# A macaron transformer block: the row maxima of two heads in one reduction, one of four transposed copies on VectorE, and the query/key rounding issued between two heads' exponentials

## The reference, cut to what matters

```python
# x: (32, 256, 128); ffn: H=16 heads, DH=64, E=8 experts, top-2
def ffn(x):                        # x already layer-normed
    q = einsum('btc,hdc->bhtd', x, Wq);  k = einsum('btc,hdc->bhtd', x, Wk)
    mix_v = top2_sigmoid_weights(einsum('btc,hec->bthe', x, Ws))
    v = einsum('bthe,bted->bhtd', mix_v, einsum('btc,edc->bted', x, Wv))
    probs = softmax(einsum('bhid,bhjd->bhij', q * DH**-0.5, k))
    attn = einsum('bhij,bhjd->bihd', probs, v)
    mask_o = top2_mask(einsum('btc,hec->bthe', x, Wd))
    return einsum('bthe,bthd,efd->bthf', mask_o, attn, Wo).sum(axis=2)
x = x + 0.5 * ffn(layernorm(x))
x = x + linear_attention(layernorm(x))      # states from k and v, out, layer norm, Wo
x = x + 0.5 * ffn(layernorm(x))
```

## Time and profile before

| | us |
|---|---|
| median of 3 runs | 2554.22 |
| the runs | 2555.17, 2553.99, 2554.22 |
| profiled execution, its own time | 2555.17 |
| its span | 2553.4 |
| granted TensorE clock, mean | 0.993 |

### The profile page before, as it was taken

One profiled execution on the slowest core, in us unless ns is written; L12 is line 12 of the kernel. 1 busy time (PEld: TensorE's weight loads), 2 busy tenths in 40 slices (PEclk: granted clock), 3 DMA queues, 4 the chain that ended last, 5 costly groups with the idle time before them and its releaser, 6 DMA issues.

```text
span 2553.4 us, 111659 instructions
## 1 busy us (share of the span) xinstructions
PE 2469.9 (97%) x45824; PEld 2321.9 (91%) x45824; DVE 1983.8 (78%) x3498; ACT 2073.2 (81%) x6373; POOL 1138.9 (45%) x1126
## 2 busy tenths in 40 slices
PE   4999999999999999999999999999999999999997
PEld 3899999999999999999999999999999999999997
DVE  4787777778877778888788787788787788887874
ACT  3888888888888888888888888888888888888885
POOL 2354545445445345344445354454453453444431
PEclk8999999999999999999999999999999999999998
DMA  4555555655656656555555556556556556556553
GB/s 130 149 154 147 144 146 140 163 151 153 162 147 158 158 152 157 146 164 148 157 159 155 155 150 166 149 154 164 146 155 158 153 157 157 152 145 156 162 155 99
DMA packets 519351, 387.58 MB, mean 152 GB/s; under 512 B 214080, under 2 KB 436160, under 8 KB 510656
## 3 DMA queue, kind: packets, MB, share of 16 engines
q1 hardware_dynamic: 518416, 379.60, 55.5%
q10 hardware_dynamic: 432, 0.85, 0.1%
HBM read 191.64 MB, written 188.74 MB: 149 GB/s over the span
## 4 chain that ended last, share of the span: by engine, by line
PE 80%; ACT 10%; issue 5%; DVE 3%; POOL 1%; DMA 1%; SPq 0%; ACTq 0%; DVEq 0%; POOLq 0%
PE psT L451 16%; PE psS L408 15%; PE psS L490 7%; PE psT L490 7%; ACT PB L758 7%; PE psT L468 6%; PE psT L470 5%; PE psT L469 5%; PE psT L463 5%; PE psT L421 5%; PE psT L435 4%; DVE NMAX L639 2%; ACT PT L846 1%; ACT QK L767 1%; DVE QK L698 1%
## 5 line engine op out<-in xcount | busy, mean ns | idle before, releaser
L758 ACT ACTIVATE PB<-psS,NMAX 128x256 f32<-128x256 f32 x2048 | 943.5, 488 | 246.5 <-DVE NMAX L639 246.5
L451 PE MATMUL psT<-V,PT 128*64 128x64 f32 x16384 | 540.4, 224 | 7.3 <-issue 7.1
L451 PEld LDWEIGHTS psT<-V,PT 128*64 128x64 f32 x16384 | 502.4, 138 | 35.1 <-issue 10.0
L698 DVE TENSOR_TENSOR QK<-psT,QK 128x512 fp32r<-128x512 f32 x512 | 341.1, 688 | 211.4 <-ACT QK L767 209.3
L639 DVE TENSOR_REDUCE NMAX<-psS 128x2 f32<-128x512 f32 x512 | 329.6, 685 | 202.9 <-PE psS L408 202.4
L758 ACT ACTIVATION_READ_ACCUMULATOR PB<-psS,NMAX 128x1 f32 x2048 | 452.6, 221 | 0.0
L408 PE MATMUL psS<-QK 64*128 64x256 f32 x6144 | 434.7, 286 | 14.8 <-ACT PT L846 13.1
L408 PEld LDWEIGHTS psS<-QK 64*128 64x128 f32 x6144 | 389.6, 186 | 63.5 <-issue 63.3
L767 ACT ACTIVATE QK<-psT 128x512 fp32r<-128x512 f32 x512 | 298.7, 622 | 84.1 <-PE psT L470 69.4
L864 POOL TENSOR_TENSOR BT<-MT,diagv 128x1024 f32<-128x1024 f32 x128 | 308.4, 2410 | 118.0 <-DMA MT<-MIXd 118.0
L641 DVE TENSOR_REDUCE NMAX<-psS 128x4 f32<-128x1024 f32 x256 | 310.9, 1214 | 0.0
(11 more groups left out here) (119 smaller groups left out, 4582.2 us busy)
## 6 DMA issues: line engine op xcount, KB each, us to landing
Vd<-VM SPq DMA_DIRECT2D x128, 512.0 KB, 3.9
V<-Vd SPq DMA_DIRECT2D x128, 512.0 KB, 5.2
AOd<-AO SPq DMA_DIRECT2D x256, 256.0 KB, 3.7
PJd<-PJ SPq DMA_DIRECT2D x64, 512.0 KB, 2.6
PR<-PJd SPq DMA_DIRECT2D x64, 512.0 KB, 4.0
MIXd<-MIX SPq DMA_DIRECT2D x64, 128.0 KB, 2.0
MT<-MIXd SPq DMA_DIRECT2D x64, 128.0 KB, 4.5
MASKd<-MASKR SPq DMA_DIRECT2D x64, 128.0 KB, 3.6
```

What stands on the lines that cost most here:

```text
L451: last = eng.matmul(M[64 * u:64 * u + 64, (t * NT + it) * DH:(t * NT + it + 1) * DH], PT[:, t, jt, cols], V[:, pm % 2, 4 * r + t, jt, :], ...
L698: eng.tensor_tensor(QK[:, 1, ab], bank("qk", m).rearrange("p (k t) -> p k t", k=2), QK[:, 0, ab].bitcast(F32), ALU.subtract).then_inc(free ...
L758: eng.activation(PB[:, ab, j, it, :], psS[:, ab, j, it, :], ACT.Exp, bias=NMAX[:, ab, j, it:it + 1], accum_out=SUM[:, p % 2, it, 4 * r + t ...
```

## The change

Three edits, in the programs of DVE and ACT.

1. On DVE, the maxima of t = 0 and t = 1 are taken by one reduction of 1024 columns in place of two of 512. `s_max` counts two a quarter instead of three, and both heads' exponentials wait for the one reduction.
2. The `PT` copy of t = 3 goes from the end of ACT's quarter to the end of DVE's quarter, behind everything else that DVE does in the quarter.
3. In quarters r = 0 and r = 3, `rounded(n)` goes from behind all eight exponentials to a place between those of t = 2 and those of t = 3. In r = 1 and 2 it stays.

PE's, POOL's and SP's programs are unchanged.

```diff
--- before.py
+++ after.py
@@ -634,11 +634,9 @@
                 q = p + 2
                 at = PICKS * q
                 if works(n):
-                    eng.wait_ge(s_score, 2 * n + 1)
-                    for j in range(2):
-                        eng.tensor_reduce(NMAX[:, 0, j, :], psS[:, 0, j, :, :], AX_X, ALU.max, negate=True).then_inc(s_max)
-                    eng.wait_ge(s_score, 2 * n + 2)
-                    eng.tensor_reduce(NMAX[:, 1, :, :], psS[:, 1, :, :, :], AX_X, ALU.max, negate=True).then_inc(s_max)
+                    for ab in range(2):
+                        eng.wait_ge(s_score, 2 * n + ab + 1)
+                        eng.tensor_reduce(NMAX[:, ab, :, :], psS[:, ab, :, :, :], AX_X, ALU.max, negate=True).then_inc(s_max)
                 if r == 0 and runs(p - 1):
                     eng.wait_ge(s_exp, 32 * p)
                     if p >= 2:
@@ -735,6 +733,11 @@
                     eng.scalar_tensor_tensor(KSUM[:, :], bk[:, :], float(T), M[:, 2 * C:2 * C + 2], ALU.mult, ALU.add).then_inc(s_ksum)
                     wait_freed(eng, "attn_gram", p - 2)
                     eng.scalar_tensor_tensor(GK[:, :], bkv[:, 0:2 * C], GRAM[:, C:C + 1], M[:, 0:2 * C], ALU.mult, ALU.add).then_inc(freed("attn_keys", p - 2))
+                if works(n):
+                    for t in (3,):
+                        wait_turned(eng, n, t)
+                        wait_full(eng, "product", n - 1)
+                        eng.tensor_copy(PT[:, t].rearrange("p n t -> p (n t)"), turned(n, t)).then_inc(was_copied(n, t))
 
         @block.scalar
         def scalar_program(eng):
@@ -745,11 +748,11 @@
             for weights, w in ((raw_g, wg), (raw_q, wq), (raw_k, wk), (raw_v, wv)):
                 eng.activation(w[:, 0, :], weights, ACT.Copy, scale=QSCALE if w is wq else 1.0).then_inc(s_whi)
 
-            def exponentials(n, ab):
+            def exponentials(n, ab, heads=(0, 1)):
                 p, r = divmod(n, 4)
-                for j in range(2):
+                eng.wait_ge(s_max, 2 * n + ab + 1)
+                for j in heads:
                     t = 2 * ab + j
-                    eng.wait_ge(s_max, 3 * n + (j + 1 if ab == 0 else 3))
                     if n >= 1:
                         wait_turned(eng, n - 1, t)
                     if r == 0 and t == 0 and p >= 2:
@@ -787,8 +790,16 @@
                     copy_values(p + 1, 0)
                 if r == 3 and runs(p + 1):
                     copy_values(p + 1, 1)
-                if works(n):
-                    exponentials(n, 1)
+                if r in (0, 3):
+                    if works(n):
+                        exponentials(n, 1, (0,))
+                    if works(n + 1):
+                        rounded(n)
+                    if works(n):
+                        exponentials(n, 1, (1,))
+                else:
+                    if works(n):
+                        exponentials(n, 1)
                 if r == 2 and runs(p + 3):
                     q = p + 3
                     wait_full(eng, "xturn", q)
@@ -807,7 +818,7 @@
                         wait_full(eng, "attn_keys", attn_pass[nth[q] - 1])
                         wait_freed(eng, "attn_keys", attn_pass[nth[q] - 1])
                     eng.activation(GRAM[:, :], bank("attn_gram", q)[:, 0:C + 1], ACT.Copy).then_inc(freed("attn_gram", q))
-                if works(n + 1):
+                if r in (1, 2) and works(n + 1):
                     rounded(n)
                 if r in (0, 1) and runs(p + 2):
                     q = p + 2
@@ -840,7 +851,7 @@
                         wait_full(eng, "attn_w", attn_pass[nth[q] - 1])
                     eng.activation(AAT[:, :], bank("attn_turn", q)[:, 0:T], ACT.Identity, bias=lnb[:, 0:1], scale=lng[:, 0:1]).then_inc(freed("attn_turn", q))
                 if works(n):
-                    for t in range(4):
+                    for t in (0, 1, 2):
                         wait_turned(eng, n, t)
                         wait_full(eng, "product", n - 1)
                         eng.activation(PT[:, t].rearrange("p n t -> p (n t)"), turned(n, t), ACT.Copy).then_inc(was_copied(n, t))
```

## The result

The changed kernel takes 2599.96 us (median of four runs, 2598.95 to 2605.38) against 2554.10 for the kernel before (2553.64 to 2555.17), 45.9 us more. Over all 18 runs of the changed kernel (2598.95 to 2606.64, median 2602.0) it is 47.9 us more: ratio 1.0187, 95% interval 1.0175 to 1.0199. Forecast was 2587.4, range 2566 to 2606.

What follows compares the result with a forecast made beforehand. PE was taken as the bound, busy 2469.9 of 2553.4 us, with ACT setting the end of some quarters. Terms summed to +33.2 us on the profiled 2555.17, or 2588.4; less 0.95 to the median, 2587.4, range 2566 to 2606.

Steps and rivals of the forecast that it cites:

- even passes, r = 0: Passes 10 to 60: ACT 0.53 us late less 0.17 slack, so PT copies and next scores +0.36 each, 26 times.
- odd passes, r = 3: Passes 9 to 59: ACT has no slack, 16 quarters +0.69 us, ten +0.2 because PE's slow spells hide the rest.
- odd passes, r = 0 and 1: Passes 11 to 59: DVE work behind POOL's BT delays ACT's L767; +0.28 us a pass, 25 times, bounds +0.1 and +0.5.
- even passes, r = 1 to 3: ACT's idle time takes up the later start (0.53 us, 0.69 in r = 3): 0, bound +0.18 in r = 3.
- passes 4 to 9: Earlier L767 shortens PE's waits for L698: -0.37 us in six r = 0, -0.2 in five r = 3 (passes 4 to 8).
- Edit 1, all of ACT's quarter 0.53 later: First exponentials wait for a 1214 ns reduction instead of 685; DVE's saved 0.156 us a quarter is worth nothing.
- Edit 2, worth nothing on ACT, +0.16 on DVE: ACT's freed 0.48 us goes into its NMAX wait; before r = 3 DVE's copy delays NMAX by 0.16, bounds 0 and 0.33.
- the work on ACT is the same: In r = 0 and 3, moving L767 0.90 us earlier in ACT's order adds no work; in r = 0 its banks are full.
- Hidden everywhere: Rival: slack hides the later start in all quarters, leaving about 8 us gained, 2546 us; chance 0.07.
- grouping: Rival: DVE's instructions are what counts, each quarter gets back 0.156 us, 40 us faster, 2514 us; chance 0.02.
- The copy held up by POOL: Rival: DVE's moved copy waits for POOL after r = 0 and 1, 77 us more, 2664 us; chance 0.03.
- Build-up into r = 2: Rival: in odd passes DVE's lateness grows from r = 0 into r = 2, 13 us more, 2600 and up; chance 0.16.

## Why the prediction was right

The sign, the mechanism and the range held; the median of four lies 12.6 us above the forecast, that of all 18 runs 14.6. The terms of the sum against the profiled executions:

| term | forecast | measured |
|---|---|---|
| even passes, r = 0 | +9.4 | +10.9 (0.42 each) |
| odd passes, r = 3 | +13.0 | +17.6 (0.68 each), and +7.2 of pauses |
| odd passes, r = 0 and 1 | +7.0 | -0.7 (-5.0 and +4.3) |
| even passes, r = 1 to 3 | 0 | +3.9, and +4.7 of pauses |
| passes 4 to 9 | -3.2 | -3.3 |
| passes 0 to 3 | +2.8 | +4.4 |
| passes 61 to 63 and tail | +4.2 | +2.5 (+3.4, and -0.9 from the last scores to the end) |
| sum | +33.2 | +47.2 of the span's +47.4 |

The sum came within 14 us partly by luck: most terms were put too low, and the one of odd r = 0 and 1 too high by 7.7. Had that one held, the median of all runs would lie near 2610, above the range.

- **Edit 1, all of ACT's quarter 0.53 later.** Right: with edit 1 alone, 0.55 more waiting a quarter and 0.53 in each class without slack. What the Trainium skill's Perfetto Trace Analysis, section Optimizing Scalar/DVE Operations, says of grouping came out by its second half: the 0.156 us a quarter saved on DVE gave nothing, and the bubble on ACT cost 2.0%.
- **Edit 2, worth nothing on ACT, +0.16 on DVE.** Right in odd r = 3 (0.14 alone, 0.09 on top of the others). The wait for `NMAX` took all of ACT's saved time: with edit 2 alone ACT is busy for 128.6 us less and waits for `NMAX` 163.8 us longer. Its other cost, behind the `BT` chain, I had right in place and not in company: 0.42 in odd r = 1 alone, 0.1 in the whole change.
- **Edit 3.** The two gains are real and near the size forecast (0.37 in passes 4 to 9). That "the work on ACT is the same" was true only because edit 1 had made ACT late; alone, L767 waits for its banks and the edit costs 1.1%. The forecast for the whole change didn't need this, my expectation for the edit alone did.
- **Odd r = 0 and 1, +0.28 a pass, bound +0.1.** Mis-sized: -0.03 measured, below the bound. Odd r = 0 came out as forecast (-0.20 each); the miss is in r = 1. Counted from the scores of r = 0, its L767 starts 0.43 later (medians), where I had 1.0 less 0.25, and the waits of L767 and the copies took 0.53 of delay, where I had 0.45.
- **The step that failed,** in a sum whose total held, is in the term of odd r = 3: "PE has a slow spell in some quarters' products ... I let ten of the 26 hide all but 0.2". All 26 are late in full, by 0.61 to 0.71 each (26 x 0.69 = 17.9 would have been the sum, 17.6 was measured), and the spells don't hide ACT's lateness, they grow by it, in the whole kernel from 9.4 to 21.8 us. They hang on when the load of `V` runs, which ACT's `VM` copies set. I had taken a wait named "issue" as a constant of PE.
- **Rivals.** Hidden everywhere, and grouping: out by the waits. The copy held up by POOL: out, since the longest of 256 copies took 0.693 us; this is what the Trainium skill, SBUF: State Buffer, section Who interferes with whom, says for such a copy. Build-up into r = 2: not seen, the median of odd r = 2 didn't move (-0.00); the time lies near where that rival had it, for another reason.
- **Signs named beforehand.** `NMAX` wait towards 500 us: 533.4. 512 reductions near 1214 ns: 1217. Odd r = 3 near 10.2: 10.19. Even r = 0 near 8.55: 8.60. Gap ahead of L546 gone: gone. Scores waiting for `PT` in many more than 38 quarters: 60, fewer than I meant; the weight loads of the scores stand still for more than 0.2 us in 212 quarters instead of 121, but the profile names `PT` for a part of them only.

## What to carry to other kernels

Ask of every instruction who waits for its first part, and whether the engine that it frees has a wait right behind it: DVE's 0.156 us and ACT's 0.48 us a quarter both went into such waits, and the lateness went to the one place where ACT had no slack. Put an operation forward only in the stages where its consumer waits for it; elsewhere it may itself come too early and hold up its engine. A delayed copy also delays the transfers behind it: look at what these meet. An engine's wait for "issue" inside a dense run can be something that moves: set it beside the packets of the "instruction" queue.

## What the runs showed of the hardware

- PE stops inside a run of small matmuls with nothing named to wait for; in pass 19 at the same matmul before and after the change, for 0.71 and 1.26 us. How long depends on when a 512 KB load runs: 21.8 us in all with the load as in the changed kernel, 12.8 with the `VM` copies 0.9 us earlier, 5.0 with the load behind that of `PR`; 9.4 and 16.1 for the kernel before with `VM` as it was and 0.9 later.
- Every one of the 259 pauses, in all 14 kernels, ends 1.20 to 1.66 us after the end of a packet of the profile's queue of kind "instruction" (16 KB each). In pass 19 such a packet takes 1.33 and 1.35 us at the end of the load of `V`, and 0.88 where the load is out of its way. That the packet holds PE's program is inferred from this and from the count.
- A load that no engine is seen to wait for can therefore cost PE time: moving it, and keeping all else, was worth 0.54%.
- A DVE copy that reads a PSUM bank and writes SBUF took 0.674 to 0.693 us over all 256 of its executions, while the instruction L716 just ahead, which takes two SBUF inputs, took 2.28 until POOL's `BT` was done:

```profile
L740 DVE COPY PT<-psT x256: 674/684/693, 61.5 to 2579.1; 128x512 f32<-128x512 f32 x128
```
